# Turning every second tile of x on VectorE and through DRAM, instead of on TensorE, in a Mamba-2 layer on Trainium2

## The reference

```
xn  = layernorm(x)                                  # 2 x 512 x 512
s   = mamba2(xn)                                    # in_proj, conv of width 4, silu, chunked scan, gate, norm, out_proj
g   = silu(W2 @ (silu(W1 @ xn) * (W3 @ xn)))        # 4-bit weights, hidden size 1376
out = x + s * g
```

```
scores = (C @ B.T) * exp(cs_l - cs_s), lower triangle
Y      = scores @ (x * dt) + (C @ previous state) * exp(cs) + x * D
state  = state * decay + (B * decay_states).T @ (x * dt)
```

## Time and profile before

| what | value |
|---|---|
| median of 3 runs | 1759.21 us (1757.86 to 1759.34) |
| the profiled execution's own time | 1758.21 us |
| its span, first to last instruction | 1756.4 us |
| PE, DVE, ACT, POOL busy | 1742.4, 1402.7, 1221.6, 1232.1 us |
| the chain that ended last | PE 94%, DVE 3%, of the span |
| transposes of x on PE (L738) | 512, in 128 groups of four |
| DMA | 122595 packets, 202.84 MB, q1 (SP's) 34.8% of 16 engines' span |

### The profile page before, as it was taken

The page is one execution under the profiler, slowest core; times in us unless marked ns, Lnnn a source line. Parts: engine busy times, 40 slices in busy tenths (PEclk is TensorE's granted clock), DMA queues, the critical chain, the costliest instruction groups (busy, mean ns, idle before and its releaser), DMA issues.

```text
span 1756.4 us, 30305 instructions
## 1 busy us (share of the span) xinstructions
PE 1742.4 (99%) x10301; PEld 1459.3 (83%) x10301; DVE 1402.7 (80%) x2211; ACT 1221.6 (70%) x2456; POOL 1232.1 (70%) x877
## 2 busy tenths in 40 slices
PE   8999999999999999999999999999999999999999
PEld 6788888888888888888888888888888888888877
DVE  7978788878878788778788788878887887868941
ACT  6986677777776777777867778767877787643320
POOL 5677777777876787677776777677777787576630
PEclk9999999999999999999999999999999999999999
DMA  5442333333333343333333333333323343236522
GB/s 196 165 131 99 116 116 112 98 123 109 134 105 94 104 135 109 108 101 117 118 102 118 116 111 108 103 109 127 123 91 103 109 135 107 76 98 175 146 78 96
DMA packets 122595, 202.84 MB, mean 115 GB/s; under 512 B 23056, under 2 KB 60560, under 8 KB 122192
## 3 DMA queue, kind: packets, MB, share of 16 engines
q1 hardware_dynamic: 120720, 197.32, 34.8%
q10 hardware_dynamic: 1728, 3.65, 0.5%
HBM read 193.57 MB, written 7.34 MB: 114 GB/s over the span
## 4 chain that ended last, share of the span: by engine, by line
PE 94%; DVE 3%; issue 1%; POOL 1%; DMA 0%; ACT 0%; SPq 0%; DVEq 0%; ACTq 0%; POOLq 0%
PE bank L143 17%; PE bank L145 16%; PE bank L144 16%; PE bank L573 10%; PE bank L609 7%; PE bank L677 7%; PE bank L679 7%; PE bank L678 6%; PE bank L888 3%; PE bank L738 3%; DVE z L1246 1%; PE bank L700 0%; DVE lm L1267 0%; PE bank L720 0%; DVE acc L1337 0%
## 5 line engine op out<-in xcount | busy, mean ns | idle before, releaser
L964 ACT ACTIVATE lm<-lm,hp 128x128 f32<-128x128 f32 x1024 | 313.1, 389 | 0.8
L1246 DVE SCALAR_TENSOR_TENSOR z<-bank,cw_all,z 128x511 f32<-128x511 f32 (+2 forms) x384 | 286.9, 747 | 13.3 <-ACT z L1000 4.2
L1611 POOL TENSOR_TENSOR conv_lo<-raw_x,conv_hi 128x512 fp32r<-128x512 f32 x124 | 203.7, 1643 | 129.4 <-ACT conv_hi L901 129.3
L143 PE MATMUL bank<-xn_hi,conv_hi 128*128 128x512 f32 x640 | 261.4, 408 | 1.9 <-DVE z L1246 1.4
L1306 DVE TENSOR_TENSOR xdt<-bank,hp 128x512 f32<-128x512 f32 x128 | 88.2, 689 | 212.4 <-PE bank L738 212.4
L145 PE MATMUL bank<-xn_hi,conv_lo 128*128 128x512 f32 x640 | 250.6, 392 | 0.0
L144 PE MATMUL bank<-xn_lo,conv_hi 128*128 128x512 f32 x640 | 249.5, 390 | 0.0
L1594 POOL TENSOR_TENSOR yt<-yt,ec 128x384 f32<-128x384 f32 x128 | 146.8, 1147 | 139.3 <-DVE ec L1315 107.9
L1280 DVE SCALAR_TENSOR_TENSOR lm<-lm,gm 128x1024 f32<-128x1024 f32 x128 | 225.3, 1760 | 7.8 <-ACT lm L964 7.2
L1578 POOL TENSOR_TENSOR y_lo<-yt,y_hi 128x512 fp32r<-128x512 f32 x128 | 180.1, 1407 | 52.4 <-ACT y_hi L1035 52.4
L143 PE MATMUL bank<-xn_hi,gate_hi 128*128 128x512 f32 x512 | 212.9, 416 | 0.0
(11 more groups left out here) (152 smaller groups left out, 4051.5 us busy)
## 6 DMA issues: line engine op xcount, KB each, us to landing
lm<-cs_d SPq DMA_DIRECT2D x128, 512.0 KB, 4.5
raw_x<-w_conv_dram SPq DMA_DIRECT2D x128, 256.0 KB, 3.5
ec<-e_d SPq DMA_DIRECT2D x256, 96.0 KB, 2.7
raw_o<-w_out_dram SPq DMA_DIRECT2D x64, 256.0 KB, 3.0
raw_g<-w_gate_dram SPq DMA_DIRECT2D x61, 256.0 KB, 3.2
raw_g<-w_conv_dram SPq DMA_DIRECT2D x16, 256.0 KB, 3.2
raw_o<-w_conv_dram SPq DMA_DIRECT2D x14, 256.0 KB, 3.4
q_raw<-w1q_dram SPq DMA_DIRECT2D x10, 256.0 KB, 3.9
```

Of the source, the lines that this page charges most:

```text
L143: pe.matmul(dst, a_hi, b_hi, start=(i == 0), stop=False)
L964: e = act.activation(lm[m % LM_BUFS][:, u, :], lm[m % LM_BUFS][:, u, :], ACT.Exp, bias=hp[bd.seq][:, Q_CS, k1, u:u + 1])
L1246: dve.scalar_tensor_tensor(dst[:, d:SEQ], src[:, 0:SEQ - d], cw_all[:, bd.group, pos, 3 - d:4 - d], dst[:, d:SEQ], ALU.mult, ALU.add).then ...
L1611: pool.tensor_tensor(conv_lo[kx % 2][:, :, :], raw_x[:, kx % 2, :].rearrange("p (k j) -> p k j", k=KT), conv_hi[kx % 2][:, :, :].bitcast(F ...
```

## The change

For the odd tiles t = 7, 9, ..., 123 (59 tiles, `by_blocks`) PE doesn't turn x. Instead:

- in odd step t-2, DVE waits for the tile's silu and turns `xt` in blocks of 32 x 32 into `z[:, 1]` (128 x 512, one instruction), at the head of the step, ahead of the products with dt and the decay
- in the same step SP, behind the load of raw weights and ahead of `load_rows`, writes `z[:, 1]` to DRAM (`xb_d`, 256 KB)
- in even step t-1, SP, behind the two loads of `ec`, loads `xdt[1]` from there in four DMAs, one for each quarter of the partitions; each run that is contiguous in DRAM has 32 values (128 bytes), so that each of the four loads has 512 runs
- in odd step t, DVE waits for these loads, makes `xw` from `xdt[1]`, then waits for its own result and multiplies `xdt[1]` by dt in place. Both now read SBUF alone, where they read the bank `ps_x` before.

PE's `two_diags` waits for the chained state (`st_done`) in place of `xw_done` before it writes `ps_x`. ACT waits for the write to DRAM before it fills `z[:, 1]` anew in even step t-1.

```diff
+BLK = P // 32
...
+def by_blocks(t):
+    return paired(t) and t % 2 == 1 and t >= TILES - 1
...
+            def blocks_out(t):
+                if by_blocks(t):
+                    sp.wait_ge(blk_done, blocks_before(t) + 1)
+                    wait(sp, xtok_in, 16 * BLK * blocks_before(t))
+                    sp.dma_start(xb_d.rearrange("g i c b j -> (g i) (c b j)"), z[:, 1, :]).then_inc(xb_out, 16)
+
+            def tokens_in(t):
+                if by_blocks(t):
+                    sp.wait_ge(xb_out, 16 * (blocks_before(t) + 1))
+                    sp.wait_ge(yd_done, t - 1)
+                    for b in range(BLK):
+                        sp.dma_start(xdt[1][32 * b:32 * b + 32, :].rearrange("i (c g j) -> i c g j", c=NC, g=BLK),
+                                     xb_d[:, :, :, b].rearrange("g i c j -> i c g j")).then_inc(xtok_in, 16)
...
+                blocks_out(n + 2)
                 load_rows(body, k)
...
+                tokens_in(n + 1)
                 bd, k1 = at(body, k, 1)
...
-                pe.wait_ge(xw_done, n + 1)
+                if by_blocks(n):
+                    pe.wait_ge(st_done, n)
+                else:
+                    pe.wait_ge(xw_done, n + 1)
                 diag(n, ps_x)
...
-                if bd.exists():
+                if bd.exists() and not by_blocks(n + 1):
                     pe.wait_ge(xs_done, TILES * bd.n + k1 + 1)
...
+                    if by_blocks(m - 2):
+                        act.wait_ge(xb_out, 16 * (blocks_before(m - 2) + 1))
...
+                if by_blocks(n + 2):
+                    dve.wait_ge(xs_done, n + 3)
+                    dve.transpose(z[:, 1, :], xt[:, (k + 2) % 4, :]).then_inc(blk_done, 1)
+
                 if body.exists():
+                    if by_blocks(n):
+                        dve.wait_ge(xtok_in, 16 * BLK * (blocks_before(n) + 1))
+                        dve.wait_ge(st_mm, n)
+                        dve.tensor_tensor(by_head(xw[:, :]), by_head(xdt[1][:, 0:(NC - 1) * P]),
+                                          per_token(hp[body.seq], Q_DEC, k, NC - 1), ALU.mult).then_inc(xw_done, 1)
+                        dve.wait_ge(xw_done, n + 1)
+                        dve.tensor_tensor(by_head(xdt[1][:, :]), by_head(xdt[1][:, :]),
+                                          per_token(hp[body.seq], Q_DT, k, NC), ALU.mult).then_inc(xdt_done, 1)
+                    else:
+                        dve.wait_ge(tx_done, n + 1 - blocks_before(n))
...
```

More of the change, by code:

```diff
@@ L111, in paired, with blocks_before @@
     return TILES // 2 <= n < TILES * (BODIES - 1) + TILES // 2
+def by_blocks(t):
+    return paired(t) and t % 2 == 1 and t >= TILES - 1
+def blocks_before(t):
+    return sum(1 for u in range(t) if by_blocks(u))
 def group_exists(group):
@@ L166, in build @@
     hp_d = nc.dram_tensor("hp_d", (SEQS, P, NQ, GROUPS, TILES, 2 * NC), F32).ap()
+    xb_d = nc.dram_tensor("xb_d", (BLK, 32, NC, BLK, 32), F32).ap()
     mamba_d = nc.dram_tensor("mamba_d", (TT, P, DIM), F32).ap()
@@ L316, in build @@
         tx_done = sem("tx_done")
+        blk_done, xb_out, xtok_in = sem("blk_done"), sem("xb_out"), sem("xtok_in")
         xdt_done, xw_done = sem("xdt_done"), sem("xw_done")
@@ L432, in load_rows @@
                                  .partition_broadcast(P)).then_inc(row_in[m % LM_BUFS], 16)
+            def blocks_out(t):
[10 more added lines that the diff above has]
+                                     xb_d[:, :, :, b].rearrange("g i c j -> i c g j")).then_inc(xtok_in, 16)
             def step(body, k):
+                n = TILES * body.n + k
                 bx, kx = at(body, k, 5)
@@ L1298, in step @@
                                       None, ALU.add).then_inc(rs_done, 1)
+                if by_blocks(n + 2):
+                    dve.wait_ge(xs_done, n + 3)
+                    dve.transpose(z[:, 1, :], xt[:, (k + 2) % 4, :]).then_inc(blk_done, 1)
                 if body.exists():
[L1302 to L1310, removed]
+                    if by_blocks(n):
[8 more added lines that the diff above has]
+                        dve.wait_ge(tx_done, n + 1 - blocks_before(n))
+                        if k == 0:
+                            wait_hp(dve, body)
+                        wait(dve, yd_done, n - 1)
+                        dve.tensor_tensor(by_head(xdt[n % 2][:, :]), by_head(ps_x[:, :]),
+                                          per_token(hp[body.seq], Q_DT, k, NC), ALU.mult).then_inc(xdt_done, 1)
+                        wait(dve, st_mm, n)
+                        dve.tensor_tensor(by_head(xw[:, :]), by_head(ps_x[:, 0:(NC - 1) * P]),
+                                          per_token(hp[body.seq], Q_DEC, k, NC - 1), ALU.mult).then_inc(xw_done, 1)
                 if pv.exists():
```

## The result

| | before | after |
|---|---|---|
| median | 1758.69 us (4 runs, 1757.86 to 1759.34) | 1773.53 us (4 runs, 1772.81 to 1774.44) |
| span of the profiled execution | 1756.4 us | 1771.6 us |

The ratio is 1.0084, with a 95% interval from 1.0069 to 1.0099: the change makes the kernel slower by 14.8 us. The forecast was 1771.

What follows compares the result with a forecast made beforehand. PE, 99% busy, was taken as the bound, with DVE close behind in k = 1 and 3. 1758.2 + 10.1 (DVE's delays net of PE's savings) + 1.5 (loads) = 1769.8, said as 1771 us; range 1749 to 1803.

Steps and rivals of the forecast that it cites:

- PE is the bound and gains 0.44 us per tile: PE, busy 99% of the span: leaving out four transposes saves 0.44 us per tile, 26.0 us over 59 tiles.
- The gain in k = 0: Transposes left out for the tiles of k = 1: 0.44 us gained per tile, as for the other tiles.
- D: DVE ahead of L1315 in odd steps: turn 0.65, lost overlap 0.1, POOL wait 0.6; 1.35 us, between 0.7 and 2.5.
- What comes out in k = 1: Change at PE, D less slack, less 0.44: 0.81 us per step in seq 0, 0.11 in seq 1; +6.6 us.
- What comes out in k = 3: Change at PE, D less slack, the 0.44 not showing: 1.35 us per step in seq 0, 0.85 in seq 1; +16.3 us.
- k = 5 and 7: Steps where D stays under DVE's 1.6 us slack: 29 tiles gain 0.44 us each, -12.8 us.
- The loads: Four loads on SP's queue: 7.3 us from first issue to last landing, about 0.1 us late at k = 7, +1.5 us.
- PE's busy time: Expected sign in the profile: PE's busy time falls by some 26 us and its waits become some 35 us.
- The rival without that wait: DVE's two products don't wait for POOL: D = 0.75, total change -5.9 us, 1753 us; chance 0.19.
- late loads: The four loads land later than 7.3 us after first issue; at 9 us, about 1803 us; chance 0.17.
- full cover: All added work hides and PE's 26.0 us come out in full: 1733 us; chance 0.05.
- a D of 2.5: Both DVE products wait for POOL and the waits add up: +45 us, 1804 us; chance 0.05.

Runs made afterwards that it cites:

- long_runs: The changed kernel with an odd tile's four loads taking contiguous 2 KB rows instead of 128-byte runs (tile order wrong): 1772.85 us, ratio 1.0082 to the kernel before.
- bank_inputs: The changed kernel with both products of the odd tiles reading the bank ps_x instead of the loaded tile (x wrong): 1757.12 us, ratio 0.9991 to the kernel before.
- no_turn: The changed kernel without DVE's transpose instruction, all DMAs, waits and products kept (x of odd tiles wrong): 1767.78 us, ratio 1.0054 to the kernel before.

## Why the prediction was right

- **PE is the bound and gains 0.44 us per tile.** Right. The gain shows in k = 2, 4 and 6 and in no other step.
- **The gain in k = 0.** Wrong: it shows 0.05 us, not 0.44. Behind the turned tile PE transposes the squares there, and that waits for POOL's sum (3.3 us of idle time in total; from the start of the last product of the step ahead of them to their own start it is 0.59 us, where 0.23 is the usual distance). I had put k = 0 with the others. It costs 15 x 0.39 = 5.9 us.
- **D, DVE's added time ahead of the product into `ec`.** 1.35 us was forecast from a turn of 0.65, a lost overlap of 0.1 and one wait for POOL of 0.6. In k = 1 of seq 0 it ends at 4.74 instead of 3.37 us into the step: 1.37. In k = 3, counted from the start of k = 2 because that step is shorter now, it is 1.26 in seq 1, and 1.04 in seq 0, where POOL's instruction was met by the operation on `lm` ahead (2.10 us, median) and not by `xw` (0.51). In k = 1 of seq 1 it is 0.71, without a wait: `xw` takes 0.52 us (931.88) beside POOL's operation on 128 x 4 (931.42, 1.02 us), which I had taken for one that blocks.
- **What comes out in k = 1.** The forecast was that `diag` is late by 1.25 us in seq 0; it is by 1.26. Missing was a second wait in the same step, of the state products for the second product with D, 0.73 us where it is shown above: beyond `diag`'s delay it adds 2.22 - 1.26 = 0.96 us to the step, 7 times, 6.7 us. Its cause is the operation on `lm` that now meets `conv_lo`; the prediction charged waits for POOL to the two products alone. In seq 1 I forecast 0.55 us of wait and there is none, 4.4 us too much.
- **What comes out in k = 3**, k = 2 included: +1.35 and +0.85 forecast, -0.42 + 1.41 = +0.99 and -0.46 + 1.23 = +0.77 measured; summed over the steps 12.4 us instead of 16.3. The slack of 0.0 in seq 0 was read in the tightest of seven bodies: there 0.08 us pass from L1315 to `diag`, in five others 0.16 to 0.19 and in one 0.59, so they don't all repeat within 0.1 us. When PE does wait, 0.055 us pass, not 0.08.
- **k = 5 and 7** cost nothing, as forecast: -12.8 forecast, -12.2 summed over the steps 4 to 7.
- **The loads.** I had 7.3 us to the last landing, just in time in k = 7, for 1.5 us. They land in 2.6 us each, the last 4.7 us after the first is issued, so that the spacing of some 0.7 us is that of issuing, the lower of my bounds; they cost nothing. That they have 128-byte runs doesn't matter (long_runs).
- **PE's busy time.** It was to fall by some 26 us and falls by 16.9. The records of matmuls overlap, and the one ahead of a wait counts in full, so this sum is no measure of the work taken from PE; that this makes the whole difference isn't shown.

For the steps k = 0 and 1 together 6.6 us were forecast, and the sum over the steps is 14.2. So the total is right to 3 us partly by luck, because two misses offset others: the second wait and k = 0 (+12.6) against seq 1, k = 3 and the loads (-4.4, -3.9, -1.5). The mechanism was right, and bank_inputs shows which part of it is the largest: the wait for POOL's instruction. The rival without that wait (1753 us) lies 4 us below what bank_inputs measures when the wait is taken away, 1757.1 us; it priced a case that isn't this one. The rivals of late loads and of full cover are refuted by the idle time of 0.0 ahead of `xw` and by the 25.0 us that PE waits.

That the second product would meet a POOL instruction as well didn't happen in k = 1 and 3 of the changed kernel, where a D of 2.5 would have counted. It did in k = 5: the multiplication by dt takes 1.66 us in all 14 of these steps, and 0.69 in the other 45, at no cost, since DVE has time to spare there. Where the turn is left out it is common: in no_turn the multiplication has a median of 1654 ns, against 692.

What stays open: why POOL's instruction comes before or after DVE's in k = 3 of seq 0. It depends on tenths of a microsecond, and I have read the outcome, not a rule.

## What to carry to other kernels

Where one engine is the bound and another stands behind it, read the second engine's slack at each place where the first waits for it, by step, and not its busy share: the same edit was worth -7.2 us for one quarter of the tiles and +17.4 for another. Count two due times in a step, and ask of a step whose gain is booked what its neighbour waits for next. When an operand moves from a bank to SBUF, the time of the operation may depend on what GpSimd is doing at that moment, and being late by a little can bring other operations, further on, into the same wait; then what stands ahead of it may be free, and leaving it out or moving it gains nothing or loses.

## What I had not expected of the hardware

- A DVE operation with two SBUF inputs waits for GpSimd's 512-element operations (`xw` up to 1.65 us against 0.51 to 0.56, the operation on `lm` 2.09 against 1.21), but ran in 0.52 us beside GpSimd's operation on 128 x 4, which is 1.0 us long in the profile.
- DVE's turn of 128 x 512 float32 values takes 697 to 712 ns, hardly more than L1306 (674 to 693), and isn't stretched by GpSimd, with one SBUF input.
- Loads of 512 runs of 128 bytes (64 KB) land in 2.6 us and cost 0.64 us of issuing each; with 2 KB runs it is 2.0 and 0.42 us.
